# One kernel, two orders: the segments of every engine and the FFN's turns in another sequence

## The reference

```python
x = x + attn_a(layernorm(x), Wq, Wk, Wv, Wo)          # 16 heads of 8, rotary, causal over 256
x = x + ffn(layernorm(x), w_gate, w_up, w_down)       # silu(gate)*up, 352 wide, FP4 rounding of inputs and weights
x = x + attn_b(layernorm(x), w_qkv, ln_w, w_proj)     # rmsnorm on q and k, causal inside groups of 32
x = x + ffn(layernorm(x), w_gate, w_up, w_down)       # same weights as the first FFN
```

## Time and profile before

| what | value |
|---|---|
| median of 3 runs | 606.99 us (606.18 to 609.55) |
| the profiled execution, its own time | 605.69 us |
| its span, first to last instruction | 603.9 us |
| mean granted TensorE clock, share of full | 0.815 |
| PE busy | 421.6 us, 70% |
| DVE busy | 364.0 us, 60% |
| ACT, POOL busy | 34%, 30% |

### The profile page before, as it was taken

The page is one execution under the profiler, slowest core; times in us unless marked ns, Lnnn a source line. Parts: engine busy times, 40 slices in busy tenths (PEclk is TensorE's granted clock), DMA queues, the critical chain, the costliest instruction groups (busy, mean ns, idle before and its releaser), DMA issues.

```text
span 603.9 us, 10380 instructions
## 1 busy us (share of the span) xinstructions
PE 421.6 (70%) x4061; PEld 268.8 (45%) x4061; DVE 364.0 (60%) x894; ACT 203.7 (34%) x548; POOL 179.8 (30%) x207
## 2 busy tenths in 40 slices
PE   0034577776866897889779687978878764968743
PEld 0023345454544564556555454554644342534422
DVE  3983418377585487757885769488585455062532
ACT  1010240522612642364366126524543313313310
POOL 9540200332332240442162306132324043020202
PEclk9985887778995898699989877999895858575865
DMA  7003130401451340117023303604003101300000
GB/s 233 3 26 80 46 62 2 109 0 30 80 105 34 77 105 3 30 39 149 12 80 74 63 10 107 107 5 110 6 4 92 22 3 47 68 2 10 1 9 9
DMA packets 59938, 31.04 MB, mean 51 GB/s; under 512 B 3249, under 2 KB 59505, under 8 KB 59889
## 3 DMA queue, kind: packets, MB, share of 16 engines
q1 hardware_dynamic: 59888, 30.37, 22.2%
HBM read 16.14 MB, written 13.63 MB: 49 GB/s over the span
## 4 chain that ended last, share of the span: by engine, by line
PE 54%; DVE 17%; ACT 10%; DMA 7%; POOL 5%; SPq 4%; issue 3%; POOLq 0%; DVEq 0%; ACTq 0%
PE bank L888 8%; PE bank L903 6%; PE bank L764 4%; PE bank L725 4%; PE bank L849 4%; PE bank L844 3%; PE bank L779 3%; DVE bmax L1251 3%; PE bank L693 3%; DMA Qf<-nmTf 3%; PE bank L857 2%; PE bank L896 2%; PE bank L768 2%; ACT probl L1005 2%; ACT prob L962 2%
## 5 line engine op out<-in xcount | busy, mean ns | idle before, releaser
L1251 DVE TENSOR_REDUCE bmax<-bank 128x3 f32<-128x384 f32 x128 | 63.2, 549 | 14.4 <-PE bank L749 13.7
L962 ACT ACTIVATE prob<-bank 128x384 f32<-128x384 f32 x128 | 56.4, 492 | 31.1 <-PE bank L768 30.4
L764 PE MATMUL bank<-Qf,Kf 128*128 128x256 bf16 x128 | 30.7, 330 | 30.4 <-DMA Qf<-nmTf 22.1
L1005 ACT ACTIVATE probl<-bank 128x512 f32<-128x512 f32 x64 | 38.2, 597 | 40.5 <-PE bank L849 40.0
L1332 DVE TENSOR_TENSOR xall<-bank,xall 128x128 f32<-128x128 f32 x32 | 9.3, 291 | 52.4 <-PE bank L903 52.2
L1077 POOL TENSOR_TENSOR qk<-ra,rb 128x512 f32<-128x512 f32 x8 | 11.9, 1484 | 86.8 <-DVE rb L1243 86.8
L1102 POOL TENSOR_TENSOR fb__w<-fb__w,fb__c 128x704 f32<-128x704 f32 x8 | 13.4, 1672 | 77.4 <-DVE fb__w L1213 77.4
L844 PE MATMUL bank<-maskb,identb 128*128 128x512 bf16 x64 | 28.7, 448 | 10.3 <-ACT probl L1005 7.0
L1323 DVE SCALAR_TENSOR_TENSOR fb__hg<-fb__th,bank 128x352 f32<-128x352 f32 x16 | 8.3, 518 | 43.3 <-ACT fb__th L1023 43.2
L779 PE MATMUL bank<-prob,Vf 128*32 128x128 f32 (+1 forms) x512 | 28.8, 344 | 4.3 <-ACT oTf L923 4.3
L888 PE MATMUL bank<-wguT,fb__xqT 128*128 128x352 f32 x64 | 28.1, 569 | 5.3 <-DVE fb__h L1324 3.3
(11 more groups left out here) (212 smaller groups left out, 1055.6 us busy)
## 6 DMA issues: line engine op xcount, KB each, us to landing
scr_f<-partsf SPq DMA_DIRECT2D x16, 192.0 KB, 2.4
Qf<-scr_f SPq DMA_DIRECT2D x16, 192.0 KB
Kf<-scr_f SPq DMA_DIRECT2D x16, 192.0 KB
scr_l<-partsl SPq DMA_DIRECT2D x16, 192.0 KB, 2.4
Ql<-scr_l SPq DMA_DIRECT2D x16, 192.0 KB, 3.9
Kl<-scr_l SPq DMA_DIRECT2D x16, 192.0 KB, 4.9
scr_f<-partsf SPq DMA_DIRECT2D x16, 128.0 KB, 1.9
scr_l<-partsl SPq DMA_DIRECT2D x16, 128.0 KB, 1.9
```

Source lines behind the costliest of these rows:

```text
L764: pe.matmul(ring(2 * g + j)[:, 0:256], Kf[:, g, 0:128], Qf[:, 2 * g + j, 0:256], start=True, stop=True)
L962: act.activation(prob[:, h % 8, :], bank[h % 3][:, 0:384], ACT.Exp).then_inc(f.s_exp, 1)
L1005: act.activation(probl[:, u % 2, :, :].rearrange("p c n -> p (c n)"), bank[4][:, :], ACT.Exp).then_inc(l.s_exp, 1)
L1251: dve.tensor_reduce(bmax[:, h, :], bank[h % 4][:, 0:384].rearrange("p (n k) -> p n k", k=P), AX.X, ALU.max).then_inc(bmax_done, 1)
```

## The change

No instruction is added or removed. `TIMES` has other numbers for all engines, so that the segments stand in another order, and `FFN_TURNS` lets the phases of two passes alternate from the fourth pass on. A constant `VS = 16` is added that nothing uses; line numbers after it are one higher.

```diff
@@ -35,6 +35,7 @@
 VW = 32
+VS = 16
@@ -44,12 +45,12 @@ FFN_TURNS
     ("a", 0, "up"), ("a", 0, "down"), ("a", 1, "up"), ("a", 1, "down"),
-    ("a", 2, "up"), ("a", 2, "down"), ("a", 3, "up"), ("a", 3, "down"),
-    ("b", 0, "up"), ("b", 0, "down"), ("a", 4, "up"), ("a", 4, "down"),
-    ("b", 1, "up"), ("b", 1, "down"), ("a", 5, "up"), ("a", 5, "down"),
-    ("b", 2, "up"), ("b", 2, "down"), ("a", 6, "up"), ("a", 6, "down"),
-    ("b", 3, "up"), ("b", 3, "down"), ("a", 7, "up"), ("a", 7, "down"),
-    ("b", 4, "up"), ("b", 4, "down"), ("b", 5, "up"), ("b", 5, "down"),
+    ("a", 2, "up"), ("a", 2, "down"), ("a", 3, "up"), ("b", 0, "up"),
+    ("a", 3, "down"), ("a", 4, "up"), ("b", 0, "down"), ("a", 4, "down"),
+    ("b", 1, "up"), ("a", 5, "up"), ("b", 1, "down"), ("a", 5, "down"),
+    ("b", 2, "up"), ("a", 6, "up"), ("b", 2, "down"), ("a", 6, "down"),
+    ("b", 3, "up"), ("a", 7, "up"), ("b", 3, "down"), ("b", 4, "up"),
+    ("a", 7, "down"), ("b", 4, "down"), ("b", 5, "up"), ("b", 5, "down"),
     ("b", 6, "up"), ("b", 6, "down"), ("b", 7, "up"), ("b", 7, "down"),
@@ pe.local1, batches 1 and 7
-113 116 121
+105 106 114
-387 388 389
+387 388 392
```

More of the change, by code:

```diff
@@ L61 @@
 9 10
-14 16
+15 16
 20 22
-28 30
-35 37""",
+26 28
+33 34""",
     "sp.front2": """
@@ L69 @@
 8
-13
+14
 19
-27
-34
-43""",
+25
+32
+39""",
     "sp.local1": """
@@ L78 @@
 23 24
-29 31
-36 38
+29 30
+36 37
 41 42
-45 47
-49 50""",
+45 46
+49 51""",
     "sp.local2": """
-15
+13
 21
-26
-32
-39
+27
+35
+40
 44
@@ L93 @@
     "sp.store": """
[L94 to L98, removed]
+31
+38
+43
+47
+50
 53
@@ L107 @@
 35 36
[L108 to L112, removed]
+65 67
+102 103
+148 149
+199 200
+249 251""",
     "pe.front2": """
 3 4 5 6 7 8 9 10 13 14 15 16 17 18 19 20 21 22 23 24 25 26
[6 rows of a table removed]
[L121 to L131 removed]
[7 rows of a table removed]
[L139 to L155 removed]
[6 rows of a table added]
+286 287 289 291 292 296 298 299 306 310 312 314 317 319 321 322 324 327 328 330 336 339""",
+    "pe.local1": """
+70 72 77
+105 106 114
+156 159 165
+206 208 214
+264 267 272
+316 318 323
+356 358 360
+387 388 392""",
+    "pe.local2": """
[7 rows of a table added]
+410 413 415 416 418 420 421 423 424 425 426 427 428 429""",
+    "pe.ffn_a2": """
+40 42 45 54 57 59 66
+74 75 79 88 90 91 95
+109 111 115 127 130 142 147
+161 163 166 183 188 190 195
+210 215 220 243 245 247 248
+265 269 271 294 297 301 303
+315 320 325 342 344 346 348
+357 359 361 379 381 383 384""",
+    "pe.ffn_b2": """
+172 174 179 223 226 229 231
+254 255 259 275 278 279 284
+307 308 311 332 334 337 340
+350 352 354 364 366 368 370
+372 374 377 389 390 391 393
+395 397 400 409 411 412 414
 417 419 422 430 431 432 433
@@ L216 @@
 5 6 7 8
-9 12 13 15
-16 20 21 24
-25 31 32 33
-35 44 47 50
-51 59 60 63
-65 73 74 75""",
+9 12 14 15
+16 21 22 24
+26 32 33 36
+37 43 44 47
+48 56 57 59
+60 70 71 73""",
     "pool.front2": """
@@ L226 @@
 17
-27
-38
-52
-68
-81""",
+28
+40
+52
+65
+78""",
     "pool.local1": """
-23 26 29
-36 37 41
-43 49 53
-54 58 66
-67 72 78
-80 85 86
-90 92 95
-101 102 104""",
+20 25 27
+31 35 38
+42 49 51
+55 61 64
+69 76 79
+83 85 88
+92 94 96
+100 102 104""",
     "pool.ffn_a1": """
-11 14
-19 22
+11 13
+19 23
 30 34
-40 42
-56 57
-70 71
-83 84
-94 96""",
+41 46
+54 58
+68 72
+81 82
+90 91""",
     "pool.ffn_a2": """
 18
-28
+29
 39
-45
-62
-77
-88
+53
+67
+80
+89
 98""",
     "pool.ffn_b1": """
-46 48
-61 64
-76 79
-87 89
-91 97
-99 100
+45 50
+62 66
+74 75
+84 86
+93 97
+99 103
 106 107
@@ L268 @@
     "pool.ffn_b2": """
-55
-69
-82
-93
-103
+63
+77
+87
+95
+101
 105
@@ L277 @@
     "dve.weights": """
-0 2 3 4 5 6 7 8 10 11 13 15 16""",
+1 2 3 4 5 6 7 8 10 11 12 15 16""",
     "dve.front1": """
-1 9 12
+0 9 13
 14 17 35
-36 37 59
-60 63 90
-91 98 127
-132 135 175
-186 189 228
-238 241 278""",
+36 37 60
+61 64 93
+95 100 132
+133 137 171
+173 179 218
+220 225 265""",
     "dve.front2": """
 18 19 20 21 22 23 24 25 26 27 28 29 30 31 32 33 34 38 39
[6 rows of a table removed]
-302 303 304 305 310 313 314 315 316 317 320 322 323 325 326 328 330 348 350""",
-    "dve.local1": """
-96 97 103 106
-134 136 141 144
-162 179 187 190
-191 218 232 234
-240 264 280 284
-290 291 318 321
-339 340 353 355
-376 378 382 384""",
-    "dve.local2": """
-129 168 176
-180 208 213
-219 250 254
-257 297 301
-306 334 341
-344 365 367
-370 390 392
[6 rows of a table added]
+291 292 293 294 295 296 298 299 300 301 302 303 306 307 308 309 311 333 336""",
+    "dve.local1": """
+92 94 98 101
+126 130 136 139
+167 170 181 183
+214 217 227 229
+264 266 280 282
+314 317 327 329
+345 348 356 359
+376 378 382 385""",
+    "dve.local2": """
+107 156 168
+172 205 215
+219 260 267
+271 310 315
+319 343 346
+350 369 373
+377 392 393
 395 406 407""",
     "dve.ffn_a1": """
-40 57 61 62
-71 88 92 94
-108 125 128 130
-146 151 153 155
-198 205 207 209
-249 256 258 260
-300 307 309 311
-352 356 358 360""",
-    "dve.ffn_a2": """
-64 65 66 67 69 93 95
-99 100 101 102 104 131 133
-137 138 139 140 143 152 154
-163 167 171 173 177 182 184
-220 224 226 229 231 236 239
-269 276 279 281 283 288 289
-319 324 327 329 332 337 338
-362 363 364 366 368 372 374""",
-    "dve.ffn_b1": """
-178 181 183 185
-230 233 235 237
-282 285 286 287
-331 333 335 336
-343 346 354 361
-369 371 373 375
+40 57 59 62
+71 91 96 97
+110 129 134 135
+147 169 174 176
+191 197 216 221
+240 250 263 268
+289 297 305 313
+337 339 341 342""",
+    "dve.ffn_a2": """
+63 65 66 67 68 88 90
+99 102 103 104 105 109 124
+138 140 141 142 143 145 165
+182 184 185 187 188 202 212
+230 233 235 237 239 257 262
+279 281 283 285 287 304 312
+328 330 331 332 334 340 344
+357 361 362 363 365 371 374""",
+    "dve.ffn_b1": """
+175 177 178 180
+223 228 231 232
+270 273 275 277
+316 321 323 325
+347 352 354 360
+375 380 381 383
 394 396 398 400
```

72 lines of the change are left out of this document (36 added, 36 removed), and 64 rows, old and new, of the table TIMES.

## The result

| | before | after |
|---|---|---|
| median | 606.59 us (604.8 to 609.55) | 547.44 us (545.92 to 551.1) |
| profiled execution, its span | 605.69, 603.9 us | 545.92, 543.8 us |
| mean granted clock | 0.815 | 0.881 |

The ratio is 0.903, 95% interval 0.897 to 0.909: 59 us less, where 22 were forecast, and outside the range. The median of before is here over four runs instead of three. Some executions of a kernel, slower and mostly at a lower granted clock, are left out of every ratio but not of the medians, so a ratio can differ from that of two medians.

What follows compares the result with a forecast made beforehand. It took the waits of PE, the busiest engine with its stream in order, as the bound. 8 + 11 + 3 = 22 us off the profiled 605.69 gave 583.7, median 585.0; range 570 to 602.

Steps and rivals of the forecast that it cites:

- 115 to 450 us: Long middle of the kernel: PE waits filled or removed, less newly opened waits; net 8 us less.
- place A: Batches 3, 5 and 6: other PE work between the maxima's transpose and their scores; 6.1 us less, bounds 4 and 10.6.
- place B: Batch 6: SP issues the read of `Kf` ahead of the `partsl` writes, so PE's wait goes; 2.7 us less.
- attention-output chains: End of `front2`, batches 3 and 5 to 7: transpose, normalise, project waits filled; 3 us less, bounds 1 and 5.
- new waits: Five places with less work between producer and consumer than before; 5 us more, from a range of 2 to 7.5.
- 450 to 548 us: Stretch before the kernel's end: six longer PE waits filled or shortened; net 11 us less, bounds 6 and 13.
- place C: Last `xnl` row: batch 4's down phase fills the `qkn` and `restl` waits; 3.8 of 4.46 us and 1.50 go.
- The clock: Two low-clock stretches behind the 3.07 and 4.46 us waits: shorter waits save 3 us, bounds -3 and 13.
- DVE becomes the pace: 115 to 450 us: DVE contends with POOL and grows 11 us; 599 us, chance 0.17, plus 0.06 for no change.
- The turns bind: FFN phases: seven must wait for a phase of the other FFN, costing 31 us; 616 us, chance 0.07.
- Nothing happens: Whole kernel: PE work moved into one wait leaves as long a wait elsewhere; no change, within a chance of 0.06.
- The clock comes up too: First of the rivals: 450 to 548 us runs fast, clock gives 13 us, first part 10; 573 us, chance 0.15.

Runs made afterwards that it cites:

- waits_filled: Kernel before, turns unchanged, with only the predicted waits filled (maxima in batches 3, 5, 6; `Qf` and `Kf` reads ahead of local writes): 598.55 us, ratio 0.998.
- old_alt_ls: Placement of before with the new alternating FFN turns, rearranged by a rule that takes the segment able to start first: 599.58 us, ratio 0.996.
- tail_old: Kernel after up to the last `xnl` row, from there the order of before on every engine: 556.22 us, ratio 0.921.
- filler_old: Kernel before with nine added matmuls that nothing reads, at the maxima waits of batches 0, 1, 2, 3, 5 and 6: 592.18 us, ratio 0.988.
- serial_ls: Placement of after with the serial FFN turns of before, rearranged by a rule that takes the segment able to start first: 611.9 us, ratio 1.020.

## Why the prediction was wrong

**What bounds the kernel now: the step that failed.** "No engine is full, so the waits of PE, whose stream is in order, decide" took each wait of PE, as it stands in the timeline, for time that can be won in the middle. Filling such waits brought nothing (`waits_filled`, 0.998). What decides there is when a pass of an FFN gets banks 6 and 7 and whether its input is there by then: with the placement of after, the order of the turns is worth 41 us (611.9 to 571.1), with that of before nothing (599.9 and 599.6). I read `FFN_TURNS` only as a source of waits, never as something that is handed round with a busy time of its own, and so saw neither the beat of 59.5 us nor how late the inputs come. That the turns alone set this beat is not shown: it stays at 56 to 66 us in `old_alt_ls`, where they are opened. The bound that I gave, "at most 66.1 + 28.6 = 94.7 us of PE idleness is open", would have held the 34.5 us of idle time that went; it says nothing of the 25.6 us of busy time.

**115 to 450 us, 8 us: mis-sized since its mechanism was the wrong one, and with the clock put at nothing.** To the last `xnl` row it was 52.8: 30.4 us of idle time, where 8 were forecast, and 22.4 of busy time, for which this part had no term at all. The parts:

| part | forecast | trace after |
|---|---|---|
| maxima, place A | 6.1 | batches 3, 5 and 6: 10.6 to 4.7, so 5.9; all eight: 22.1 to 17.5, so 4.6 |
| `Kf`, place B | 2.7 | 10.4 to 7.6: 2.8 |
| attention-output chains | 3 | L792 3.6 to 0.9: 2.7 on one of three steps |
| DVE order | 1 | L746 for `bmax` 4.1 to 3.3, for `xall` 1.8 to 0.6: 2.0 |
| new waits | -5 | `local2(0)` waits 4.26 for `Kl` instead of 2.41, batch 4's maxima 2.06 instead of 0.82 |

The waits were read well, and `waits_filled` shows that A and B are worth nothing that can be measured by themselves: in the order of before the time came back as waits for `bmax` and `prob`. The timeline after at batch 3's maxima, against the earlier trace rows, shows place A at work:

```profile
189.51 0.28 PE L699 MATMUL bank<-identb,npartf 128*128 128x128 bf16 x2
...
190.48 1.56 PE L807 MATMUL bank<-wqkvb,xnTl 128*128 128x384 f32 x4 [0.47 <-ACT xnTl L924]
...
193.67 0.39 PE L765 MATMUL bank<-Qf,Kf 128*128 128x256 bf16 x2 [1.63 <-DMA Qf<-nmTf]
```

**450 to 548 us, 11 us: right in place C, where it can be compared.** From the last `xnl` row on it was 7.9 us, and `tail_old` confirms it with 7 to 11. I had 3.8 of the 4.46 and all of the 1.50: 0.58 is left of the one and 0.22 of the other. The 1.75 us of `fb__u` and the 1.66 for `fb__h` are gone. The 2.17 of `fa__u` is 0.88, now a wait for the turn, and the 3.07 of the other `qkn` is 2.63, where 1.4 less was counted. The clock stood at 0.65 behind the last `xnl` row and is at 0.77; in the 19 us behind the last wait for `qkn`, the sign named for the first rival, it stood at 0.50 and is at 0.86.

**The clock, 3 us with bounds -3 and 13: too small.** The same matmuls take 25.6 us less, 22.4 of it in the first stretch. There the granted clock was 0.87, but the term looked only behind 450, and there at two low stretches, 39 us together; yet by the means of the earlier trace rows some 68 of the 98 us from 450 to 548 were at the lower level (at 0.50 all of 535 to 548, behind a wait of 2.24 us for `attnl` that the prediction does not name). This is no pure clock gain of the time, as a faster PE also waits more; with the waits left in place, fills are worth 1.2% in before and 2.3% in after. My reason for the low value, that PE stayed at 0.50 though busy 88% of the time, did not carry over. The Trainium skill ("TensorE: Matmul & The Clock Gate", section "HAM oscillation — how this bites in real kernels") has waits of PE as what throws it to the lower clock, with the work behind each wait slow; `filler_old` agrees, as filling the waits raised the mean clock from 0.826 to 0.845.

**The rivals.** *DVE becomes the pace* did not come: DVE's busy time fell from 364.0 to 356.7 us. `fb__xn` still has one of 1693 ns and `fa__w` has no longer any above 893, where the earlier trace rows had 1843. The Trainium skill ("SBUF — State Buffer", section "Who interferes with whom") has one of DVE and GpSimd blocked while the other holds the pair of ports they share; no run here tests that, and whatever made those rows long cost DVE less in the new order. *The turns bind* had the right object with the wrong sign: I asked what new turn waits could cost (seven by my count, six pairs by the lists), and never what the old turns cost. *Nothing happens* names what `waits_filled` did: PE work moved into a wait left as long a wait elsewhere. *The clock comes up too* was nearest, at 573, and its sign came, but the time is 26 us below it.

**What stays open.** That the old turns are the pace on the new placement and the alternation worth 41 us there is shown, for tables made by one rule; that it is worth nothing on the old placement, and that neither half of the placement is enough, is shown too. What sets the beat of before, if not the turns alone, is open. Which rows of the table of after make the last 24 us that no rule of mine reached was not found, nor what limits after now: its beats of 45 to 36 us still fall.

## What to carry to other kernels

Before the waits of the busiest engine are priced, list for each shared resource that is handed round (PSUM banks above all) when it is taken and given back, and look for a beat: starts of the same step in successive batches that are equal to within 1%, while the work between them differs, are a sign that something passes through end to end. Then note beside every turn when the input of its user is ready. Inputs that lie ready for 30 us, as in `serial_ls`, say that the turns are the pace, and opening them brought 41 us. Inputs that come within a few microseconds of their turn, as in before, say that something else is late as well, and opening the turns brought nothing. Here, waits priced from a timeline added up at the end of the program (7.9 us) and not in its middle. And look at the clock of every stretch, not only of the one where it is lowest.
